# A macaron block of two routed FFN halves around attention: side tasks on even steps, results consumed one step later, head and tail in a new order

## The chip, the cores and the metric

The kernel runs on one core of one Trainium2 chip. Its time is the device time of one execution in microseconds. The core has a matmul engine (TensorE, PE in the profile; its weight loads are PEld), two elementwise engines that read the matmul results from PSUM (VectorE, DVE; ScalarE, ACT), a third elementwise engine (GpSimd, POOL), and a queue (SyncE, SP) that only issues DMAs. Each engine works through its own instruction list in order; semaphores tie the lists together.

## The reference, cut to what matters

```
x = L0_attn_x                                       # (4, 512, 512)
x = x + 0.5 * ffn(layernorm(x))
x = x + attn(layernorm(x))                          # 32 query heads, 8 key/value groups, head size 128
x = x + 0.5 * ffn(layernorm(x))

attn: q, k = rope(x@Wq), rope(x@Wk);  v = x@Wv
      out = softmax(causal(q k^T / sqrt(128))) v;   return out @ Wo + bo
ffn:  query = h@Wq.T;  scores = (query@Wr.T)(aux_keys@Wr.T).T / sqrt(48) + log_rel      # 128 slots
      top 8 of the slots; w = softmax of their (query.key / 8 + log_rel)
      aux = (w @ values) @ Wvd.T @ Wvu.T
      u = log1p(var(h)) / mean(log1p(var(h))) * 0.5 + sigmoid(gelu(h@Wu1.T + bu1)@Wu2.T + bu2) * 2.5
      gate = sigmoid(gate_w1 * clip((clip(u,0,5) - 0.5)/1.5, 0, 1) + gate_bias), 0 where under 0.05
      return h + gate * aux
```

## The kernel before

All of x stays in SBUF as X, 16 tiles of 128 rows by 512 columns, four tiles to a batch. Every product is made of three 16-bit matmuls (a high part and a low part of each operand, `mm3`, the lines L1047, L1048 and L1049), so almost every PSUM result is read twice: ScalarE copies the high part out, VectorE subtracts it to get the low part.

**Steps.** Attention runs as 128 steps s: 4 batches, 8 groups (a unit n is one group of one batch, 32 in all), 4 heads h, so s = 4n + h. In step s TensorE does, in this order: scores(s) (L1202 to L1204, into SC); the query projection of the head two steps on (`queries_of`); attend(s-2) (into PV), which needs the probabilities of two steps ago, turned by DMA; the side tasks of this step (`side`); and the rest (`rest_of`): at h = 1 the next unit's K projection, at h = 3 its V projection, and in every step one of the four row tiles of a unit's output projection O.

**What the other engines do in a step.** VectorE, in order: minima(s) (mask and row minimum, L863), the low parts of the probabilities of step s-1 (`p_lo`, L874, four pieces, with the reciprocal L955 among them), the rope of the query (L834 to L836), `out_lo(s-2)` (L881), then the rest of the same step, thus K's rope, or V's low part (L840), and the add of O into X (`project_add`, L850), and at the end the side tasks. ScalarE: exps(s) (L565), `out_hi(s-2)` (L557), `p_hi(s)` (L574), the high parts of the ropes (L547) and of V (L551), side tasks, and in the first batch the high parts of the weights (L541). GpSimd: the two additions of every rope (L436, L439), side tasks, and in the first batch the low parts of the weights (L429), a second subtraction over 128x512. SP: refills of weights, and for each step four transposing DMAs (`turn`, L374), each when VectorE has written that piece's low part.

**PSUM.** Every projection and every side task writes one of four banks (PJ) in turn: `RING` is the list of all those tasks in TensorE's order, and a task waits (`free`) until the task four places before it has been read (`consumed`).

**Side tasks.** While batch b is in attention, the first FFN half of batch b+1 (tables ending in _A) and the second half of batch b-1 (_B) run in between. The tables are keyed by the step within the batch, u = 0 to 31. LT turns a normalised tile (L1060) and is followed by ScalarE's high part (`hi`) and VectorE's low part (`lo`, L718); SCR, HID, HOUT, ET and AUX are the router scores, the hidden layer, its output, the turned softmax (L1099) and the product with the values. `nrm` (L712) normalises a tile, `aux` (L820) adds the FFN's result to X, `mom` (L678) takes its moments.

**Head and tail.** Before step 0 come the setup products of the FFN's weights, the first half for batch 0 (`HEAD`) and the first four projections (`FIRST`). Behind step 127 come the last output projections (`LAST`) and the second half for batch 3, with all 16 AUX products of that half (`TAIL`). In the head every engine waits for all 14 small loads at once:

```
            pe.wait_ge(ld_f, 16 * NFL)
            mm(PV[0:RDIM, 0:NSLOT], fwrT[:, :], fkeyT[:, :], start=True, stop=True).then_inc(fs_pe, 1)
```

## Time and profile before

| | us |
|---|---|
| median of 3 runs (1540.57 to 1544.21) | 1541.02 |
| the profiled execution | 1551.33 |
| its span, from the first to the last instruction | 1549.5 |
| TensorE busy | 1420.2 |
| VectorE busy | 1222.1 |
| ScalarE busy | 882.3 |
| GpSimd busy | 527.7 |

The profile is of one execution. Busy is the time in which an engine had an instruction under way; the rest is idle, and the profile says which event ended an idle time. The granted clock is TensorE's clock as a share of 2.4 GHz: 0.5 is the level of 1.2 GHz. A row of the timeline merges instructions of one line that follow each other (x4), and gives in brackets the idle time before the first and what ended it.

### The profile page before, as it was taken

Reading aid. Unit: us, or ns where it says so; the run is one execution under the profiler, and the core shown is the slowest. Engines: PE = TensorE matmul, PEld = TensorE weight load, DVE = VectorE, ACT = ScalarE, POOL = GpSimd, SP = SyncE. Lnnn points to the kernel's source line nnn. Section 1 sums busy time; section 2 is a strip of 40 time slices with the busy share of each in tenths; the row PEclk is TensorE's granted clock in tenths of the full one; section 3 lists DMA queues with packets and bytes.
Section 4 is the critical chain, followed back from the end, with each engine's and each line's share of the span. In section 5 each row is a group of like instructions: output and inputs, shape, how many; then the busy total and the mean of one; then the engine's idle time right before and its main releaser. Section 6 shows DMA issues by size and latency. Waiting matters only on the chain.

```text
span 1549.5 us, 26280 instructions
## 1 busy us (share of the span) xinstructions
PE 1420.2 (92%) x8962; PEld 800.1 (52%) x8962; DVE 1222.1 (79%) x3119; ACT 882.3 (57%) x2170; POOL 527.7 (34%) x441
## 2 busy tenths in 40 slices
PE   3487998999999999999899999999899999999966
...
GB/s 220 41 67 183 178 156 166 187 188 163 168 140 144 126 118 99 129 115 112 116 139 129 124 106 112 136 107 110 113 139 134 135 133 134 125 113 120 105 52 109
DMA packets 409539, 201.12 MB, mean 130 GB/s; under 512 B 352160, under 2 KB 353376, under 8 KB 409408
## 3 DMA queue, kind: packets, MB, share of 16 engines
...
## 4 chain that ended last, share of the span: by engine, by line
PE 70%; DVE 13%; ACT 6%; issue 4%; POOL 3%; SPq 2%; DMA 2%; POOLq 0%; ACTq 0%; DVEq 0%
PE PJ L1047 16%; PE PJ L1049 16%; PE PJ L1048 16%; PE PV L1047 4%; PE PV L1049 4%; PE PV L1048 4%; PE SC L1202 3%; PE SC L1203 3%; PE SC L1204 3%; ACT p L565 3%; DVE phl L874 2%; POOL t L436 2%; DVE p L863 2%; DMA pTf<-phl 1%; DVE t L836 1%
## 5 line engine op out<-in xcount | busy, mean ns | idle before, releaser
L436 POOL TENSOR_TENSOR t<-t 128x512 f32<-128x512 f32 x160 | 202.9, 1268 | 744.5 <-DVE t L836 744.3
L565 ACT ACTIVATE p<-p,mn 128x512 f32<-128x512 f32 (+3 forms) x512 | 281.7, 553 | 191.2 <-DVE mn L863 191.0
L874 DVE SCALAR_TENSOR_TENSOR phl<-p,ri,phl 128x512 f16<-128x512 f32 (+3 forms) x512 | 292.7, 595 | 0.0
L574 ACT ACTIVATE phl<-p,ri 128x512 f16<-128x512 f32 (+3 forms) x512 | 245.1, 552 | 14.8 <-DVE ri L959 12.0
L1047 PE MATMUL PJ<-XTh,wsp 128*128 128x512 f16 x640 | 244.3, 382 | 1.4 <-DVE XTl L718 1.4
L1048 PE MATMUL PJ<-XTl,wsp 128*128 128x512 f16 x640 | 244.1, 381 | 0.0
L1049 PE MATMUL PJ<-XTh,wsp 128*128 128x512 f16 x640 | 244.1, 381 | 0.0
L1047 PE MATMUL PJ<-wosp,oTf 128*128 128x512 bf16 x512 | 197.4, 386 | 29.8 <-issue 24.4
L863 DVE CUSTOM_DVE_ANT_0 p<-SC,maskw 128x512 f32<-128x512 f32 (+3 forms) x512 | 220.0, 485 | 4.9 <-PE SC L1204 3.1
L1049 PE MATMUL PJ<-wosp,oTl 128*128 128x512 bf16 x512 | 197.7, 386 | 0.0
L1048 PE MATMUL PJ<-wosp,oTf 128*128 128x512 f16 x512 | 197.3, 385 | 0.0
L1047 PE MATMUL PV<-pTf,vh 128*128 128x512 f16 (+3 forms) x512 | 157.0, 307 | 26.6 <-DMA pTf<-phl 26.6
L439 POOL TENSOR_TENSOR qTl<-t,qTh 128x512 f16<-128x512 f32 x128 | 148.2, 1158 | 94.3 <-ACT qTh L547 94.3
L547 ACT CAST qTh<-t 128x512 bf16<-128x512 f32 x128 | 79.1, 618 | 150.3 <-POOL t L436 150.3
L850 DVE TENSOR_TENSOR X<-PJ,X 128x512 f32<-128x512 f32 x128 | 88.1, 689 | 93.0 <-PE PJ L1049 93.0
L1048 PE MATMUL PV<-pTf,vh 128*128 128x512 f16 (+3 forms) x512 | 157.2, 307 | 0.0
L1203 PE MATMUL SC<-kTl,qTh 128*128 128x512 f16 (+3 forms) x512 | 154.1, 301 | 0.0
L1049 PE MATMUL PV<-pTf,vl 128*128 128x512 f16 (+3 forms) x512 | 150.9, 307 | 0.0
L1202 PE MATMUL SC<-kTh,qTh 128*128 128x512 bf16 (+3 forms) x512 | 147.8, 302 | 2.8 <-POOL qTl L439 2.8
L1204 PE MATMUL SC<-kTh,qTl 128*128 128x512 bf16 (+3 forms) x512 | 147.3, 300 | 0.0
L557 ACT ACTIVATE oTf<-PV 128x512 bf16<-128x512 f32 x128 | 75.6, 591 | 114.1 <-PE PV L1049 114.0
L1049 PEld LDWEIGHTS PJ<-XTh,wsp 128*128 128x128 f16 x640 | 62.9, 98 | 76.6 <-issue 2.1
...
## 6 DMA issues: line engine op xcount, KB each, us to landing
...
pTf<-phl SPq DMA_TRANSPOSE x512, 2.9
...
```

The source lines that it names most:

```text
L436: nc.gpsimd.tensor_tensor(t1[:, j, :], t1[:, j, :], t2[:, j, :], ALU.add).then_inc(rope_sum, 1)
L439: nc.gpsimd.tensor_tensor(lo, t1[:, j, :], hi, ALU.subtract).then_inc(rope_lo, 1)
L565: ins = nc.scalar.activation(pt, pt, ACT.Exp, bias=mn[:, par, i:i + 1], scale=-1.0, accum_out=rs[:, par, i:i + 1])
L574: nc.scalar.activation(phl[:, par, POFF[i]:POFF[i] + w], p[:, par, SOFF[i]:SOFF[i] + w], ACT.Copy, scale=ri[:, par, i:i + 1]).then_inc(a_p ...
L863: ins = nc.vector.tensor_tensor_reduce(out=p[:, par, SOFF[i]:SOFF[i] + w], in0=SCf[:, SOFF[i]:SOFF[i] + w], in1=maskw[:, T - w:T], scale=1 ...
L874: nc.vector.scalar_tensor_tensor(out=phl[:, par, POFF[i] + w:POFF[i] + 2 * w], in0=p[:, par, SOFF[i]:SOFF[i] + w], scalar=ri[:, par, i:i + 1],
L1047: mm(out_, lh, rh, start=start, stop=False)
L1048: mm(out_, lh, rl, start=False, stop=False)
L1049: return mm(out_, ll, rh, start=False, stop=stop)
L1202: mm(o, qh, kh, start=True, stop=False)
L1203: mm(o, qh, kl, start=False, stop=False)
L1204: ins = mm(o, ql, kh, start=False, stop=True)
```

## The change

Five things change together.

- VectorE, ScalarE and GpSimd take what TensorE projected in the rest of step s (K, V, O) in step s+1 (`rest_before`), ahead of the query's rope; TensorE's own order keeps K at h = 1 and V at h = 3, and O comes one step later than before, so the wait for `o_lo` of a unit's last head stands at h = 2.
- TensorE's side tasks stand on even steps alone, mostly two at a time. Tiles go through two buffers per half (`hb` and the unused `asc`).
- The head: the small loads have five semaphores in the order of use and the weights' loads wait for the third quarter of x; the products for the scores come first, those for the values behind the first turned tiles; the moments of tiles 4 to 15 are spread between other work on VectorE; GpSimd's penalty goes before the weights' low parts and its bias adds behind the first ropes; ScalarE spreads the weights' high parts; V's projection goes behind the first query's.
- The end of the loop: the last unit's output projections do three of four heads before the last attend, and the fourth behind it.
- The tail: the hidden layer goes first, the gates of all 16 tiles are made in one pass, VectorE takes tile 15 too, and the last quarter of the output is stored as two halves.

```diff
-PE_A = {2: [("LT", 0, 0)], 3: [("LT", 0, 1)], 4: [("LT", 0, 2)], 6: [("LT", 0, 3)], 7: [("SCR", 0, 0)],
-        8: [("HID", 0, 0)], 10: [("SCR", 0, 1)], 11: [("HOUT", 0, 0)], 14: [("ET", 0, 0)],
-        16: [("AUX", 0, 0)], 18: [("AUX", 0, 1)], 19: [("AUX", 0, 2)], 20: [("AUX", 0, 3)],
-        23: [("LT", 1, 0)], 24: [("LT", 1, 1)], 26: [("LT", 1, 2)], 27: [("LT", 1, 3)]}
-PE_B = {9: [("LT", 2, 0)], 12: [("LT", 2, 1)], 13: [("LT", 2, 2)], 15: [("LT", 2, 3)], 17: [("SCR", 1, 0)],
-        18: [("HID", 1, 0)], 21: [("SCR", 1, 1)], 22: [("HOUT", 1, 0)], 25: [("ET", 1, 0)]}
...
+PE_A = {2: [("LT", 0, 0), ("LT", 0, 1)], 4: [("LT", 0, 2), ("LT", 0, 3)], 6: [("SCR", 0, 0)], 8: [("SCR", 0, 1)],
+        10: [("HID", 0, 0)], 12: [("HOUT", 0, 0), ("ET", 0, 0)], 18: [("AUX", 0, 0), ("AUX", 0, 1)],
+        20: [("AUX", 0, 2), ("AUX", 0, 3)], 24: [("LT", 1, 0), ("LT", 1, 1)], 26: [("LT", 1, 2), ("LT", 1, 3)]}
+PE_B = {12: [("LT", 2, 0), ("LT", 2, 1)], 14: [("LT", 2, 2), ("LT", 2, 3)], 16: [("SCR", 1, 0)], 22: [("SCR", 1, 1)],
+        28: [("HID", 1, 0)], 30: [("ET", 1, 0), ("HOUT", 1, 0)]}
...
+DVE_A = {0: [("nrm", 0, 0), ("nrm", 0, 1)], 2: [("lo", 0, 0), ("lo", 0, 1), ("nrm", 0, 2), ("nrm", 0, 3)],
+         4: [("lo", 0, 2), ("lo", 0, 3)], 6: [("scr", 0, 0)], 7: [("top", 0, 0)], 8: [("scr", 0, 1)],
+         9: [("top", 0, 1)], 10: [("min", 0, 0)], 12: [("hout", 0, 0), ("g1", 0, 0), ("et", 0, 0)],
+         14: [("g2", 0, 0)], 16: [("g3", 0, 0)],
+         18: [("aux", 0, 0), ("mom", 1, 0), ("aux", 0, 1), ("mom", 1, 1)],
+         20: [("aux", 0, 2), ("mom", 1, 2), ("aux", 0, 3), ("mom", 1, 3), ("var", 1, 0)],
+         22: [("std", 1, 0), ("nrm", 1, 0), ("nrm", 1, 1)],
+         24: [("lo", 1, 0), ("lo", 1, 1), ("nrm", 1, 2), ("nrm", 1, 3)], 26: [("lo", 1, 2), ("lo", 1, 3)]}
...
+def rest_before(s):
+    return rest_of(*divmod(s - 1, HG)) if s else []
+
+
 def queries_of(n, h):
     q = (n, h + 2) if h < 2 else (n + 1, h - 2)
     return [("Q",) + q + (0,)] if q[0] < NU else []
 
 
 def rest_of(n, h):
-    r = {0: [("O", n - 2, 3, 0)], 1: [("K", n + 1, 0, 0), ("O", n - 1, 0, 0)], 2: [("O", n - 1, 1, 0)],
-         3: [("V", n + 1, 0, 0), ("O", n - 1, 2, 0)]}[h]
+    r = {0: [("O", n - 2, 2, 0)], 1: [("K", n + 1, 0, 0), ("O", n - 2, 3, 0)], 2: [("O", n - 1, 0, 0)],
+         3: [("V", n + 1, 0, 0), ("O", n - 1, 1, 0)]}[h]
     return [t for t in r if 0 <= t[1] < NU]
...
-FIRST = [("K", 0, 0, 0), ("V", 0, 0, 0), ("Q", 0, 0, 0), ("Q", 0, 1, 0)]
-LAST = [("O", NU - 2, 3, 0)] + [("O", NU - 1, i, 0) for i in range(4)]
...
+FIRST = [("K", 0, 0, 0), ("Q", 0, 0, 0), ("V", 0, 0, 0), ("Q", 0, 1, 0)]
+LAST = [("O", NU - 2, 2, 0), ("O", NU - 2, 3, 0)] + [("O", NU - 1, i, 0) for i in range(4)]
+TAIL = ([("LT", 2, 3, i) for i in range(4)] + [("HID", 1, 3, 0), ("MEAN", 1, 0, 0), ("SCR", 1, 3, 0), ("SCR", 1, 3, 1),
+        ("HOUT", 1, 3, 0)] + [("AUX", 1, 0, i) for i in range(4)] + [("AUX", 1, 1, 0), ("AUX", 1, 1, 1), ("ET", 1, 3, 0),
+        ("AUX", 1, 1, 2), ("AUX", 1, 1, 3)] + [("AUX", 1, b, i) for b in range(2, 4) for i in range(4)])
...
-REFILL = {0: [(1, "Q1"), (1, "V")], 1: [(1, "Q2"), (0, "W0")], 2: [(1, "Q3"), (2, "K"), (0, "W1")],
-          3: [(2, "Q0"), (0, "W2"), (0, "W3")]}
-HEAD_ITEMS = [(0, "K"), (0, "V"), (0, "Q0"), (0, "Q1"), (0, "Q2"), (0, "Q3"), (1, "K")]
+REFILL = {0: [(1, "Q1"), (1, "V"), (-1, "W3")], 1: [(1, "Q2")], 2: [(1, "Q3"), (2, "K"), (0, "W0")],
+          3: [(2, "Q0"), (0, "W1"), (0, "W2")]}
+HEAD_ITEMS = [(0, "K"), (0, "Q0"), (0, "V"), (0, "Q1"), (0, "Q2"), (0, "Q3"), (1, "K")]
...
+            for dst, src in ((fwrT[:, :], f_wrT), (fkeyT[:, :], f_keyT), (fwr[:, :], f_wr)):
+                sp.dma_start(dst, src).then_inc(ld_fr, 16)
+            sp.dma_start(fwq, f_wq).then_inc(ld_fq, 16)
+            sp.dma_start(fwu1T, f_wu1T.rearrange("(c p) n -> p c n", p=P)).then_inc(ld_fu, 16)
+            for dst, src in ((fvalT, f_valT.rearrange("(c p) n -> p c n", p=P)),
+                             (fwvdT[:, :, :], f_wvdT.rearrange("(c p) n -> p c n", p=P)), (fwvuT, f_wvuT)):
+                sp.dma_start(dst, src).then_inc(ld_fv, 16)
...
+            sp.wait_ge(ld_x[2], 16)
+            for r in range(4):
+                raw_load(r)
+            for dst, src in ((ck[:, :], cosk), (sk[:, :], sink), (cq[:, :], cosq), (sq[:, :], sinq),
+                             (bob[:, :], bo.to_broadcast([P, C]))):
                 sp.dma_start(dst, src).then_inc(ld_t, 16)
...
+            for c0, c1 in ((0, 4), (4, 8), (8, 12), (12, 14), (14, 16)):
+                sp.wait_ge(r_xd[1], evens(c1))
+                sp.wait_ge(r_xp[1], c1 - evens(c1))
+                sp.dma_start(out_v[:, c0:c1, :], X[:, c0:c1, :]).then_inc(st_out, 16)
+            sp.wait_ge(st_out, 16 * 5)
...
+            penalty(0, 0)
             for r in range(6):
                 weight_low(r)
-            penalty(0, 0)
-            for i in range(4):
-                add_bias(0, i)
             for kind, n, idx, _ in FIRST:
                 if kind in "QK":
                     rope(kind, n, idx)
             weight_low(6)
+            for i in range(4):
+                add_bias(0, i)
...
-            act.wait_ge(ld_f, 16 * NFL)
+            for c in range(CC):
+                act.wait_ge(fs_pe, 3 + c)
+                nc.scalar.copy(ah[:, c, :], setup_bank(c)).then_inc(fs_hi, 1)
+            root(0, 0, 0, 4)
+            act.wait_ge(ld_fu, 16)
             nc.scalar.copy(uh[:, :, :], fwu1T).then_inc(fs_hi, 1)
-            for c in range(CC):
-                act.wait_ge(fs_pe, 5 + c)
-                nc.scalar.copy(ah[:, c, :], SC[:, c % 2, 0:2 * NSLOT]).then_inc(fs_hi, 1)
...
             for i in range(4):
                 turned_hi(0, 0, i)
+            act.wait_ge(fs_pe, 8)
+            nc.scalar.copy(v2h[:, :], PV[:, :]).then_inc(fs_hi, 1)
+            for i in range(4):
                 base(0, 0, i)
+            act.wait_ge(ld_fs, 96)
+            gelu(0, 0)
+            logs(0)
+            exps_ffn(0, 0)
+            weight_high(0)
+            e_hi(0, 0)
...
             root(0, 1, 4, NT)
-            logs(0)
-            gelu(0, 0)
-            for r in range(6):
-                weight_high(r)
-            exps_ffn(0, 0)
-            gate_exp(0, 0, 4)
-            e_hi(0, 0)
-            gate_exp(1, 0, 4)
+            weight_high(2)
             root(1, 0, 0, 4)
+            weight_high(3)
             for i in range(4):
                 turned_hi(1, 0, i)
+            weight_high(4)
+            weight_high(5)
...
+                for kind, m, _, _ in rest_before(s):
+                    if kind == "V":
+                        value_hi(m)
                 if s >= 2:
                     out_hi(s - 2)
                 p_hi(s)
-                for kind, m, idx, _ in queries_of(n, h) + rest_of(n, h):
-                    if kind in "QK":
-                        rope(kind, m, idx)
-                    if kind == "V":
-                        value_hi(m)
+                for kind, m, _, _ in rest_before(s):
+                    if kind == "K":
+                        rope("K", m, 0)
+                for _, m, idx, _ in queries_of(n, h):
+                    rope("Q", m, idx)
...
+            gelu(1, bb)
             for i in range(4):
                 base(2, bb, i)
-            gelu(1, bb)
+            gate_exp(8, 0, NT)
+            gate_exp(9, 0, NT)
...
+            dve.wait_ge(fs_pe, 2)
+            nc.vector.tensor_copy(rmat[:, :], PJ[0:BOT, 2, 0:NSLOT]).then_inc(fs_ev, 1)
             for n in range(4):
-                moments(0, n)
...
+                setup_lo(c)
             deviation(0, 0, 0, 4)
             for i in range(4):
                 normal(0, 0, i)
...
                 turned_lo(0, 0, i)
...
+            dve.wait_ge(fs_pe, 7)
+            nc.vector.tensor_copy(u1T[:, :], SC[0:VB, 0, 0:NSLOT]).then_inc(fs_ev, 1)
+            dve.wait_ge(ld_fs, 96)
+            for n in range(6, 10):
+                arrived(n)
+            take_scores(0, 0, 0)
+            top(0, 0, 0)
+            arrived(10)
+            take_scores(0, 0, 1)
+            top(0, 0, 1)
+            for n in range(11, NT):
+                arrived(n)
             variance(0, 4, NT)
             dve.wait_ge(ln_v[0], 2)
             variance_logs(0)
...
+            minima_ffn(0, 0)
+            dve.wait_ge(fs_hi, 6)
+            nc.vector.tensor_tensor(v2l[:, :], PV[:, :], v2h[:, :], ALU.subtract).then_inc(fs_lo, 1)
...
+            e_lo(0, 0)
             gate_2(0, 0, 0, 4)
-            e_lo(0, 0)
-            gate_3(0, 1, 0, 4, 1)
+            gate_3(0, 1, 0, 4)
+            scales(0, 0, 4, 1)
...
                 nc.vector.tensor_scalar_mul(ri[:, par, :], ri0[:, :], PSCALE).then_inc(d_norm, 1)
                 if s:
                     p_lo(s - 1, 3)
-                for kind, m, idx, _ in queries_of(n, h):
-                    rope(kind, m, idx)
-                if s >= 2:
-                    out_lo(s - 2)
-                for kind, m, idx, _ in rest_of(n, h):
+                for kind, m, idx, _ in rest_before(s):
                     if kind == "K":
                         rope(kind, m, idx)
                     if kind == "V":
                         value_lo(m)
                     if kind == "O":
                         project_add(m, idx)
+                for kind, m, idx, _ in queries_of(n, h):
+                    rope(kind, m, idx)
+                if s >= 2:
+                    out_lo(s - 2)
...
+            for _, m, idx, _ in rest_before(NS):
+                project_add(m, idx)
             for k in range(TB):
                 p_lo(NS - 1, k)
             out_lo(NS - 2)
+            for _, n, i, _ in LAST[:2]:
+                project_add(n, i)
             out_lo(NS - 1)
-            for _, n, i, _ in LAST:
+            for _, n, i, _ in LAST[2:]:
                 project_add(n, i)
...
+            learned(1, bb)
+            gate_1(1, 0, NT, 4)
             top(1, bb, 0)
+            gate_2(1, 8, 0, NT)
             take_scores(1, bb, 1)
...
+            gate_3(1, 9, 0, NT)
+            scales(1, 0, 12, 3)
...
+            for n in (6, 8, 10, 12, 14, 15):
...
+            pe.wait_ge(ld_fr, 48)
+            mm(PJ[0:RDIM, 3, 0:NSLOT], fwrT[:, :], fkeyT[:, :], start=True, stop=True).then_inc(fs_pe, 1)
             pe.wait_ge(fs_ev, 1)
-            mm(SC[0:BOT, 2, 0:NSLOT], fwr[:, :], rk[:, :], start=True, stop=True).then_inc(fs_pe, 1)
+            mm(PJ[0:BOT, 2, 0:NSLOT], fwr[:, :], rk[:, :], start=True, stop=True).then_inc(fs_pe, 1)
...
+            for c in range(CC):
+                mm(setup_bank(c)[:, 0:NSLOT], fwq[:, c * P:(c + 1) * P], rmat[:, :], start=True, stop=True)
+                mm(setup_bank(c)[:, NSLOT:2 * NSLOT], fwq[:, c * P:(c + 1) * P], fkeyT[:, :],
+                   start=True, stop=True).then_inc(fs_pe, 1)
+            pe.wait_ge(cst, 1)
+            for task in HEAD[:4]:
+                ffn_task(task)
+            pe.wait_ge(fs_lo, 4)
+            pe.wait_ge(ld_fv, 48)
...
+            for task in HEAD[4:6]:
+                ffn_task(task)
             pe.wait_ge(fs_ev, 3)
-            for c in range(CC):
-                if c >= 2:
-                    pe.wait_ge(fs_lo, c)
-                mm(SC[:, c % 2, 0:NSLOT], fwq[:, c * P:(c + 1) * P], rmat[:, :], start=True, stop=True)
...
+            pe.wait_ge(fs_lo, 5)
+            ffn_task(HEAD[6])
+            pe.wait_ge(ld_fs, 96)
...
+            for kind, n, idx, _ in LAST[:2]:
                 project(kind, n, idx)
+            pe.wait_ge(o_lo, NS - 1)
+            for h in range(HG):
+                piece_ready(NU - 1, f"W{h}")
+            for task in LAST[2:]:
+                free(task)
+                project_out(NU - 1, task[2], range(HG - 1))
             attend(NS - 1)
-            for kind, n, idx, _ in LAST[1:]:
-                project(kind, n, idx)
+            pe.wait_ge(o_lo, NS)
+            for task in LAST[2:]:
+                project_out(NU - 1, task[2], range(HG - 1, HG)).then_inc(s_o, 1)
```

## Rows read from the trace of the kernel before

**Rows 1.** Stretches: length, busy of PE, PEld, DVE, ACT, POOL; clock, DMA share, GB/s.
```profile
0.00:99.17 99.17, 47.50 (x233) 29.89 (x233) 51.38 (x142) 26.50 (x49) 20.13 (x25) 0.83 0.30 102
99.17:164.38 65.21, 52.23 (x288) 28.52 (x289) 51.70 (x116) 44.38 (x106) 37.04 (x31) 0.87 0.69 174
164.38:455.09 290.71, 275.32 (x1761) 152.98 (x1760) 248.97 (x581) 187.68 (x461) 157.71 (x130) 0.98 0.68 169
455.09:807.39 352.30, 341.40 (x2221) 193.72 (x2220) 289.55 (x753) 206.54 (x516) 106.12 (x88) 1.00 0.52 123
807.39:1161.59 354.20, 344.09 (x2221) 194.50 (x2220) 289.23 (x753) 206.53 (x516) 104.26 (x86) 0.99 0.53 119
1161.59:1470.31 308.72, 307.00 (x1985) 172.47 (x1984) 251.55 (x658) 183.06 (x469) 91.07 (x75) 1.00 0.55 125
1470.31:1508.18 37.87, 25.95 (x122) 12.05 (x120) 17.81 (x48) 9.51 (x21) 0.00 (x0) 0.91 0.28 59
1508.18:1549.50 41.32, 26.75 (x138) 15.92 (x138) 21.91 (x69) 18.07 (x33) 11.40 (x9) 0.79 0.28 102
```

**Rows 2.** TensorE's waits, whole span: line, released by: us in total, times, longest.
```profile
PE PV L1047 <- DMA pTf<-phl: 26.6, 13, 4.5
PE PJ L1047 <- issue: 24.4, 13, 3.9
PE PV L1209 <- DMA lrb<-in_f_lr: 21.3, 1, 21.3
```

**Rows 3.** VectorE's waits, whole span.
```profile
DVE X L850 <- PE PJ L1049: 93.0, 84, 3.7
DVE vl L840 <- ACT vh L551: 58.7, 32, 2.5
```

**Rows 4.** Stretch of one unit without side tasks (steps 96 to 99).
```profile
1161.59:1200.62 39.03, 39.03 (x253) 21.62 (x252) 32.62 (x82) 22.14 (x58) 12.15 (x10) 1.00 0.56 135
```

**Rows 5.** The page: turning DMAs, count, us from issue to landing.
```profile
pTf<-phl SPq DMA_TRANSPOSE x512, 2.9
```

**Rows 6.** Timeline from step 104's to step 105's minima: start, us, engine, line, operation.
```profile
1242.74 0.69 DVE L863 CUSTOM_DVE_ANT_0 p<-SC,maskw 128x512 f32<-128x512 f32 x1
...
1244.38 1.28 DVE L874 SCALAR_TENSOR_TENSOR phl<-p,ri,phl 128x512 f16<-128x512 f32 x2
...
1249.92 0.68 DVE L863 CUSTOM_DVE_ANT_0 p<-SC,maskw 128x512 f32<-128x512 f32 x1
...
1245.16 5.40 SPq L374 DMA_TRANSPOSE pTf<-phl  x4
```

**Rows 7.** DMA issues of the head: count, KB each, median us to landing.
```profile
fkeyT<-in_f_keyT SPq DMA_DIRECT2D x1, 32.0 KB, 7.4
```

**Rows 8.** Timeline of the head, all engines; in brackets the idle time before.
```profile
35.44 3.65 PE L1060 MATMUL PJ<-ident,pTf 128*128 128x128 f32 x16 [4.02 <-DVE pTf L712]
...
41.35 7.21 DVE L678 BATCH_NORM_STATS2 st<-X 128x6 f32<-128x512 f32 x12
...
51.49 1.28 ACT L510 ACT_TABLE_LOAD   x1
...
52.79 0.69 ACT L510 ACTIVATE gT<-PJ,bu 128x512 f32<-128x512 f32 x1
...
54.07 6.96 POOL L429 TENSOR_TENSOR wsp<-raw,wsp 128x512 f16<-128x512 f32 x6 [51.74 <-ACT wsp L541]
...
82.88 0.58 PE L1047 MATMUL PJ<-XTh,wsp 128*128 128x512 f16 x1 [1.45 <-DVE XTl L718]
...
99.17 0.61 PE L1202 MATMUL SC<-kTh,qTh 128*128 128x512 bf16 x1 [2.82 <-POOL qTl L439]
```

**Rows 9.** VectorE's low parts in batch 0, GpSimd busy with weights.
```profile
246.65 2.87 DVE L874 SCALAR_TENSOR_TENSOR phl<-p,ri,phl 128x512 f16<-128x512 f32 x2
```

**Rows 10.** Timeline of the tail: GpSimd's last adds into X.
```profile
1540.36 3.85 POOL L467 TENSOR_TENSOR X<-X,t 128x512 f32<-128x512 f32 x3 [1.25 <-ACT t L657]
```

More of the change, by code:

```diff
@@ new lines @@
+DVE_B = {6: [("var", 2, 0)], 8: [("std", 2, 0), ("nrm", 2, 0), ("nrm", 2, 1)],
+         12: [("lo", 2, 0), ("lo", 2, 1), ("nrm", 2, 2), ("nrm", 2, 3)], 14: [("lo", 2, 2), ("lo", 2, 3)],
+         16: [("scr", 1, 0)], 17: [("top", 1, 0)], 22: [("scr", 1, 1)], 23: [("top", 1, 1)], 24: [("min", 1, 0)],
+         30: [("et", 1, 0), ("hout", 1, 0)]}
+ACT_A = {2: [("hi", 0, 0), ("hi", 0, 1)], 3: [("xup", 0, 0), ("xup", 0, 1)], 4: [("hi", 0, 2), ("hi", 0, 3)],
+         5: [("xup", 0, 2), ("xup", 0, 3)], 10: [("gelu", 0, 0)], 11: [("exp", 0, 0)], 12: [("et", 0, 0)],
+         13: [("gexp", 0, 0)], 15: [("gexp", 0, 1)], 21: [("root", 1, 0)], 24: [("hi", 1, 0), ("hi", 1, 1)],
+         26: [("hi", 1, 2), ("hi", 1, 3)]}
@@ L124, in refills @@
     out = [(1, "Q0")] if s == 0 else []
-    return out + [(n + d, kind) for d, kind in REFILL[h] if n + d < NU]
+    if s == NS - 1:
+        out = [(NU - 1, "W3")]
+    return out + [(n + d, kind) for d, kind in REFILL[h] if 0 <= n + d < NU]
 ITEMS = list(HEAD_ITEMS)
@@ L260, in rope_index, with evens @@
             return 5 * n if kind == "K" else 5 * n + idx + 1
+        odd = [1, 3, 5, 7, 9, 11, 13]
         def odd_tile(f, n):
-            return f == 1 and n % 2 == 1
+            return f == 1 and n in odd
+        def evens(n):
+            return n - len([m for m in odd if m < n])
         def consumed(task):
@@ L469, in _ @@
             penalty(1, B - 1)
-            for n in range(1, NT, 2):
+            for n in odd:
                 aux_add(n)
@@ L613, in _ @@
                 p_hi(s)
-                for kind, m, idx, _ in queries_of(n, h) + rest_of(n, h):
-                    if kind in "QK":
-                        rope(kind, m, idx)
-                    if kind == "V":
-                        value_hi(m)
+                for kind, m, _, _ in rest_before(s):
+                    if kind == "K":
+                        rope("K", m, 0)
+                for _, m, idx, _ in queries_of(n, h):
+                    rope("Q", m, idx)
                 for stage, k, bb, i in side(ACT_A, ACT_B, s):
@@ L658, in aux_odd @@
                                      scale=gs[:, 1, n:n + 1]).then_inc(r_xa[1], 1)
-            for n in range(1, 8, 2):
+            for n in odd[:3]:
                 aux_odd(n)
             exps_ffn(1, bb)
-            gate_exp(10, 12, NT)
             e_hi(1, bb)
-            gate_exp(11, 12, NT)
-            for n in range(9, NT, 2):
+            for n in odd[3:]:
                 aux_odd(n)
@@ L906, in _ @@
                 normal(0, 0, i)
+            dve.wait_ge(fs_hi, 5)
+            nc.vector.tensor_tensor(ul[:, :, :], fwu1T, uh[:, :, :], ALU.subtract).then_inc(fs_lo, 1)
+            arrived(4)
+            arrived(5)
             for i in range(4):
                 turned_lo(0, 0, i)
-            for n in range(4, NT):
-                if n % 4 == 0:
-                    dve.wait_ge(ld_x[n // 4], 16)
-                moments(0, n)
+            dve.wait_ge(fs_pe, 7)
[9 more added lines that the diff above has]
+            for n in range(11, NT):
+                arrived(n)
             variance(0, 4, NT)
@@ L1134, in halves, with project_out @@
                 return w[:, 0, :].bitcast(BF16), w[:, 1, :]
+            def project_out(n, idx, heads):
+                ts = lo_slice(idx)
+                for h in heads:
+                    wh, wl = halves(f"W{h}", n)
+                    ins = mm3(bank(("O", n, idx, 0)), oTh[:, n % 2, h, ts], oTl[:, n % 2, h, ts], wh, wl,
+                              h == 0, h == HG - 1)
+                return ins
             def project(kind, n, idx):
```

171 lines of the change are left out of this document (64 added, 107 removed).

## The prediction, made before the changed kernel was run

> **What bounds the kernel now.** I read the busy time by stretch first, then who waited for whom, then the timeline of the worst places. TensorE is busy 1420 of 1549.5 us (the PE column of [rows 1] added up), 92%, so only the rest of the span and the time at the slow clock can be won. I cut the span at the first scores of steps 0, 6, 32, 64, 96 and 127 and at the tail's first turned tile. The loss of a stretch is its idle time plus its length times (1 - granted clock), since at 1.2 GHz work takes twice as long. By [rows 1] that is, for steps 0 to 5, 13.0 + 8.5 = 21.5 us; steps 6 to 31, 15.4 + 5.8 = 21.2; batch 1, 10.9 (its clock is 1.00 as rounded); batch 2, 10.1 + 3.5 = 13.6; batch 3, 1.7; from step 127 to the tail 11.9 + 3.4 = 15.3; together 84. The head before step 0 is 99.2 us with TensorE busy for 47.5, and the tail 41.3. Thus some 225 us lie outside TensorE's bound; the middle is at it: a unit without side tasks takes 39.03 us with TensorE busy for 39.03 [rows 4].
>
> The waits say why the loop loses. TensorE waits 26.6 us for turned probabilities, and 24.4 us under "issue" at first matmuls of output projections, the longest 3.9 us [rows 2]. VectorE waits 93.0 us for the O it has to add, in 84 places, and 58.7 us at V's low part for ScalarE's high part [rows 3]. TensorE makes both at the end of a step, so an in-order engine stands still behind them, with side tasks and the next minima queued. VectorE is busy 32.6 of the 39.0 us of a clean unit [rows 4] and 290 of 352 in batch 1 [rows 1]: once it has stood still it is late, `out_lo` too, and two steps on the probabilities are late.
>
> **Units of time.** A clean unit is 180 matmuls of 512 columns or their equal (4 scores and 4 attends of 7.5 each, 10 projections of 12), so one is 39.03 / 180 = 0.217 us [rows 4], a projection 2.6, scores or an attend 1.6. Even steps are 8.4, odd ones, with K or V, 11.1. VectorE's step is 1249.92 - 1242.74 = 7.2 us if nothing waits [rows 6]: rope 2.1 (three of 0.7), `out_lo` 0.6, an add 0.6, and 3.9 for minima and low parts.
>
> **Part A, the head up to step 0.** The first product needs fkeyT, fwrT and fwr. These are now the first three issues; fkeyT takes 7.4 us from issue to landing [rows 7], so about 8.7 us in place of 21.3 [rows 2]. From there to the first turned tile it is 35.4 - 21.3 = 14.1 us now [rows 8]. The value products leave this path, four moments join it, as no waiting hides them any more (7.21 / 12 = 0.6 each, 2.4 in all [rows 8]); I count 9.3, so the tile comes at 18.0 and 17.4 is gained. From the tile to K's first matmul it is 82.9 - 35.4 = 47.4 us now. Twelve moments leave the path (7.2) and six weight subtractions ahead of the penalty (7.0) [rows 8]. Back come five moments and their sums (3.9, I take all of it), the router scores at the slow clock (3.9 of the up to 5.2 that 48 matmuls of 256 columns can lose), and 3.0 for the order gelu, logs, exps and the gates one behind the other: net 3.4. Query before V takes one projection, 2.6, off the way to the first scores. Sum 23.4; I take 22, range 12 to 27: a load that lands late would cut it.
>
> The switch of a function table on ScalarE shows as 1.28 us and the gelu follows at once: 51.49 + 1.28 = 52.77, and it starts at 52.79 [rows 8]. The Trainium skill ("ScalarE: Activation LUTs", What ACT_TABLE_LOAD costs) says that a switch costs about 2.66 us, as a drain follows the load. That rule speaks against the new order, which puts three switches between the hidden layer and the softmax: by it part A would gain 4 us less and the kernel come out at 1483. The trace shows no such drain, so the sum does not hold it.
>
> **Part B, steps 0 to 5.** VectorE is busy 51.7 of 65.2 us [rows 1] while the pipeline fills. In the change its waits for V's high part, up to 2.5 us each [rows 3], and for O go, and one O moves to the end. Of the 21.5 lost I leave 14.5, a gain of 7. Bounds: 0 if the chain of scores, exps, low parts and DMA is all there is, 14 if only the slow clock's part stays.
>
> **Part C, steps 6 to 31.** The same, with weights prepared beside it. Two low parts take 2.87 us while GpSimd subtracts, against 1.28 [rows 6, 9]. Every subtraction stays (6.96 / 6 = 1.16 each [rows 8]), and at h = 2 GpSimd now holds two ropes and three weights, about 2 x 2.4 + 3 x 1.16 = 8.3 us, which reaches into the next step's low parts. So VectorE stays near the bound: of 21.2 I leave 9, a gain of 12, range 5 to 18.
>
> Two low parts beside GpSimd's subtraction are the slower by 1.6 us [rows 6, 9]. The Trainium skill ("GPSIMD Engine Reference", 8. Key points) says GpSimd shares its SBUF interfaces with VectorE and contends with instructions of two SBUF inputs, which the low parts are. The trace agrees; if that contention alone made C's loss, all of it would stay and the kernel would come out at 1491.
>
> **Part D, batches 1 to 3.** K's rope adds 2.1 to VectorE's step and V's low part 0.6; a pair of tiles adds 1.2 for `lo`, 0.9 for `nrm`, and some 2.3 of waiting for ScalarE. At h = 2 with two tiles VectorE needs 7.2 + 2.1 + 2.1 + 2.3 = 13.7 against TensorE's 9.3, and is 4.4 late; the odd step gives back 11.1 - 7.2 = 3.9. The turning DMAs begin 2.4 us behind the minima, take 5.4 to issue and 2.9 from the last one's issue to landing: 2.4 + 5.4 - 1.35 + 2.9 = 9.4 [rows 5, 6]. TensorE wants them 4.2 into the next step, so it notices a lateness of over 12.6 - 9.4 = 3.2 us in an even step and 5.9 in an odd one. So the old waits go. New are waits in the ring of four banks, as a bank is freed a step later. At h = 2 the second tile needs K's bank, read 0.9 + 3.9 + 2.1 = 6.9 us into the step, when TensorE wants it at 1.6 + 2.6 + 1.6 + 0.5 = 6.3; with O behind it this costs 0.8, four or five times a batch. At u = 12 the ring is Q, LT, LT, HOUT, ET, O: O needs the first tile's low part, which follows the query's rope on VectorE (8.1), GpSimd (1.3) and ScalarE (2 x 0.6), at 10.6, where TensorE wants it at 8.0: with ET's wait 3 us. That makes 6 to 7 a batch, against 10.9 and 13.6 now and up to 2 of clock that the rounding hides. Gain 7 in each less 2 for batch 3, which has next to nothing to give: 12 in all, range 0 to 24.
>
> **Part E, step 127 to the tail, 37.9 us.** 15.3 of it is lost [rows 1]. Ahead of attend(127) TensorE now has three heads of the last four O, 4 x 9 x 0.217 = 7.8 us, which covers a wait for probabilities (at most 4.5 [rows 2]); behind it VectorE is the limit with four adds and four moments, 4 x 1.3. One O of 2.6 more is done here. I take 5, range 1 to 9.
>
> **Part F, the tail, 41.3 us.** GpSimd's last add ends at 1540.36 + 3.85 = 1544.2 [rows 10] and the last store takes the 5.3 us to the end. Half its size saves about 1.3; one add fewer on GpSimd (3.85 / 3 = 1.3) and one gate pass fewer (1.5) help; but the gates now wait for the hidden layer. I take 4, range -2 to 8.
>
> **Sum.** 22 + 7 + 12 + 12 + 5 + 4 = 62. Against its own execution: 1551.3 - 62 = 1489.3, with a span of 1487.5. The median of the runs is 10.3 under the profiled execution, so 1541 - 62 = 1479.
>
> **The rivals.**
> The loop gives nothing: each wait removed comes back as a bank's, or VectorE catches up and waits for O as before, which is also the case in which the change does not do what it says. For it: u = 12 and the contention of batch 0. Against: 151 us of VectorE's waits are for results that will be a step old. Left are A + E + F = 31: 1510.
>
> The loop gives nearly all: VectorE's 6.4 us of slack a unit take up the side work. B 12, C 19, D 22, with A 22 and 14 for E and F: 89, thus 1452.
>
> The head gives half: a load or ScalarE's order eats it, A 10: 1491.
>
> Slower: K's rope (2.1) and an add (0.6) now stand in an even step ahead of the query's rope; if VectorE enters even steps over 3.2 us late, each unit pays these 2.7 us on TensorE's path: 31 x 2.7 = 84 less the 62, thus 1563. For it: 4.4 late and 3.9 back do not quite cancel. Against: units with two pairs of tiles are few, and a clean one gives back more.
>
> **How the numbers follow.** Forecast 58%, loop nothing 12%, loop all 17%, head half 10%, slower 3%. The likeliest is 1479. The range of 1450 to 1512 holds all but the slower case and the outer parts of the others, some 15%. Measurement tells 0.3%, 4.6 us, from no change: faster 0.965, same 0.01, slower 0.025.
>
> **What would show it.** The first product at about 9 us and the first scores at 75 to 80 (A). VectorE's waits at the add of O and at V's low part nearly gone, and no long "issue" at O (B to D); batches 1 and 2 at 343 to 347 us each, with a wait at u = 12 that VectorE's `lo` ends (D); no wait at attend(127) (E). It is wrong if the first scores come after 87 us, or if batches 1 and 2 stay over 350 or come out at 339, where only their work is left.

## The result

The changed kernel takes 1529.25 us (median of 4 runs, 1528.1 to 1531.99) against 1541.65 for the kernel before: ratio 0.992, 95% interval 0.9901 to 0.9939, clear of the noise though under 1%. It is 12 us faster where 62 were forecast, and outside the range of 1450 to 1512. The profiled execution took 1528.1 us with a span of 1525.9.

I cut the changed kernel's span at the same places as [rows 1]: first scores of steps 0, 6, 32, 64, 96 and 127, and the tail's first turned tile.

Stretches of the changed kernel: length, busy of PE, PEld, DVE, ACT, POOL; clock, DMA share, GB/s.
```profile
0.00:72.48 72.48, 40.12 (x232) 27.79 (x235) 50.19 (x140) 26.58 (x49) 14.52 (x20) 0.86 0.42 140
72.48:136.42 63.94, 48.68 (x277) 27.64 (x280) 50.63 (x115) 42.53 (x103) 39.97 (x32) 0.89 0.65 161
136.42:431.32 294.90, 272.07 (x1729) 151.58 (x1755) 262.96 (x584) 185.94 (x460) 161.03 (x129) 0.98 0.71 169
431.32:783.78 352.46, 340.84 (x2190) 193.88 (x2221) 293.89 (x754) 206.92 (x520) 110.01 (x90) 0.99 0.54 123
783.78:1136.22 352.44, 340.54 (x2189) 193.68 (x2220) 290.96 (x753) 205.10 (x517) 104.65 (x86) 0.99 0.55 120
1136.22:1444.59 308.37, 305.47 (x1954) 172.28 (x1984) 255.59 (x658) 183.59 (x472) 93.51 (x76) 1.00 0.57 126
1444.59:1483.22 38.63, 26.71 (x131) 12.80 (x132) 18.76 (x51) 8.87 (x19) 0.00 (x0) 0.91 0.26 60
1483.22:1525.90 42.68, 25.43 (x136) 15.57 (x138) 20.31 (x57) 15.64 (x29) 10.10 (x8) 0.86 0.27 99
```
Against [rows 1] the head gave 26.7 us and steps 0 to 5 gave 1.3. Steps 6 to 31 took back 4.2. Batch 1 stands still, batch 2 gave 1.8, batch 3 0.3, and the last two stretches took back 2.1. The sum is 23.6, the whole difference of the two spans; the medians differ by 12, as the profiled execution of before was a long one. A second one of the same kernel had a head of 95.2, 289.0 us for steps 6 to 31 and a span of 1543.7, so read single stretches to 2 us, and the head to 4.

In the loop the waits of [rows 2] and [rows 3] are nearly gone, as forecast, and others stand in their place.

Waits of the changed kernel, whole span: us in total, times, longest. TensorE first (left out: 19.1 us, in the head and tail, for VectorE to normalise tiles), then VectorE, and last VectorE's wait for the scores in the kernel before.
```profile
PE PV L1102 <- DMA pTf<-phl: 18.2, 11, 3.2
PE PJ L1268 <- DMA fwr<-in_f_wr: 9.3, 1, 9.3
PE PJ L1115 <- DVE t L877: 7.9, 8, 1.7
PE PJ L1102 <- DVE t L877: 6.5, 4, 3.8
PE PJ L1115 <- DVE vl L881: 6.0, 3, 3.4
PE PJ L1103 <- DVE raw L756: 5.9, 2, 2.9
PE PJ L1154 <- DVE vl L881: 4.0, 1, 4.0
...
DVE p L904 <- PE SC L1263: 97.6, 57, 3.8
DVE ri L1007 <- ACT p L588: 57.5, 38, 4.9
DVE X L891 <- PE PJ L1104: 6.2, 4, 2.1
```
```profile
DVE p L863 <- PE SC L1204: 3.1, 3, 2.2
```
L1115 turns a tile, L1154 turns the scores, L1102 begins a projection and L1103 is another of its three matmuls. The last five of TensorE's lines are waits for a bank of PJ that VectorE has not finished reading: after K's rope (t, L877), V's low part (vl, L881), a tile's low part (raw, L756). VectorE's waiting did not vanish either. It moved from O (93.0 us, now 6.2) and V's high part (58.7, now 3.1) to the scores (3.1, now 97.6) and ScalarE's exps (19.8, now 57.5).

The costliest kind of step is that with h = 2 and two tiles. Step 58 (u = 26 of batch 1) starts at 717.51. Timeline of TensorE, then VectorE: start, us, engine, line, operation; in brackets the idle time before and its releaser.
```profile
723.37 0.61 PE L1115 MATMUL PJ<-ident,hb 128*128 128x128 f32 x4
725.70 0.65 PE L1115 MATMUL PJ<-ident,asc 128*128 128x128 f32 x4 [1.73 <-DVE t L877]
726.65 0.38 PE L1103 MATMUL PJ<-wosp,oTf 128*128 128x512 f16 x1 [0.30 <-DVE X L891]
```
```profile
718.47 0.69 DVE L904 CUSTOM_DVE_ANT_0 p<-SC,maskw 128x512 f32<-128x512 f32 x1 [0.75 <-PE SC L1263]
...
722.76 0.18 DVE L1007 RECIPROCAL ri<-rs 128x4 f32<-128x4 f32 x1 [1.36 <-ACT p L588]
...
724.96 0.68 DVE L877 TENSOR_TENSOR t<-PJ,sk 64x512 f32<-64x512 f32 x1
725.67 0.69 DVE L891 TENSOR_TENSOR X<-PJ,X 128x512 f32<-128x512 f32 x1
```
K was ready before the step began. Its bank is read to the end at 725.64, 8.1 us into the step; VectorE stood idle for 0.75 us before the minima and for 1.36 before the reciprocal, with K's rope queued behind both.

### The profile page after: what moved, and what is told of

Its sections match the earlier page's. It is cut to its first block, busy times and chain, and to the rows that moved or that the text cites. A ratio compares the mean times of both kernels' runs of the same rounds, so it can differ in the third digit from the quotient of the medians.

```text
span 1525.9 us, 26148 instructions
## 1 busy us (share of the span) xinstructions
PE 1399.9 (92%) x8832; PEld 795.2 (52%) x8962; DVE 1243.3 (81%) x3107; ACT 875.2 (57%) x2166; POOL 533.8 (35%) x440
## 4 chain that ended last, share of the span: by engine, by line
PE 61%; DVE 19%; ACT 11%; issue 4%; POOL 4%; DMA 1%; SPq 0%; DVEq 0%; ACTq 0%
PE PJ L1103 15%; PE PJ L1104 14%; PE PJ L1102 13%; ACT p L588 5%; DVE phl L915 3%; POOL t L457 3%; PE SC L1263 3%; PE SC L1261 3%; PE SC L1262 3%; PE PV L1102 3%; PE PV L1104 3%; PE PV L1103 3%; DVE p L904 2%; DVE t L877 2%; DVE t L876 2%
## 5 line engine op out<-in xcount | busy, mean ns | idle before, releaser
L915 DVE SCALAR_TENSOR_TENSOR phl<-p,ri,phl 128x512 f16<-128x512 f32 (+3 forms) x512 | 315.9, 640 | 0.0
L904 DVE CUSTOM_DVE_ANT_0 p<-SC,maskw 128x512 f32<-128x512 f32 (+3 forms) x512 | 220.1, 486 | 98.0 <-PE SC L1263 97.6
L1102 PE MATMUL PJ<-XTh,wsp 128*128 128x512 f16 x640 | 243.1, 380 | 3.4 <-DVE t L877 1.6
L1103 PE MATMUL PJ<-XTl,wsp 128*128 128x512 f16 x640 | 242.8, 379 | 0.0
L1103 PE MATMUL PJ<-wosp,oTf 128*128 128x512 f16 x512 | 197.9, 387 | 16.5 <-DVE raw L756 5.9
L1104 PE MATMUL PJ<-wosp,oTl 128*128 128x512 bf16 x492 | 190.0, 386 | 0.0
L1102 PE MATMUL PV<-pTf,vh 128*128 128x512 f16 (+3 forms) x512 | 154.1, 301 | 19.5 <-DMA pTf<-phl 18.2
L1102 PE MATMUL PJ<-wosp,oTf 128*128 128x512 bf16 x415 | 160.4, 387 | 2.5 <-DVE oTl L922 1.4
L1103 PE MATMUL PV<-pTf,vh 128*128 128x512 f16 (+3 forms) x512 | 154.5, 302 | 0.0
L922 DVE SCALAR_TENSOR_TENSOR oTl<-PV,oTf 128x512 f16<-128x512 f32 x128 | 88.6, 692 | 16.7 <-ACT oTf L580 12.8
```

The source lines that it names most:

```text
L904: ins = nc.vector.tensor_tensor_reduce(out=p[:, par, SOFF[i]:SOFF[i] + w], in0=SCf[:, SOFF[i]:SOFF[i] + w], in1=maskw[:, T - w:T], scale=1 ...
L915: nc.vector.scalar_tensor_tensor(out=phl[:, par, POFF[i] + w:POFF[i] + 2 * w], in0=p[:, par, SOFF[i]:SOFF[i] + w], scalar=ri[:, par, i:i + 1],
L1102: mm(out_, lh, rh, start=start, stop=False)
L1103: mm(out_, lh, rl, start=False, stop=False)
L1104: return mm(out_, ll, rh, start=False, stop=stop)
```

## The experiments

My theory after the result: the loop gains nothing because results are consumed behind the minima and low parts of the next step, so that banks come free late. Rival: VectorE, or its contention with GpSimd, has no room for even steps with two tiles. Each ratio is to the kernel before, timed beside the run.

**The kernel before again.** Nothing edited.

> The kernel before, unchanged, for a second profile and to see how far a profiled execution may lie from the median. If the first profile of it (1551.3 us) was an outlier of some 10 us, this one should show about 1541 with the difference in batch 0, where the traffic is heaviest; if profiling itself costs 10 us, it shows 1551 again.

Measured: 1543.94 us, ratio 1.0012 (0.9992 to 1.0032). Batches 1 and 2 take 352.9 and 353.8 us.

**The old loop.** Tables, `rest_of`, REFILL and the reading of K, V and O of the kernel before; head and tail new:
```
-for kind, m, idx, _ in rest_before(s): ...   # ahead of the query's rope
 for kind, m, idx, _ in queries_of(n, h): rope(kind, m, idx)
 if s >= 2: out_lo(s - 2)
+for kind, m, idx, _ in rest_of(n, h): ...    # behind out_lo, in the same step
```
The even-step tables and the late reading are taken back together here; no run takes back the tables alone.

> The changed kernel with the loop of before (its tables, its one-step-earlier O, its refills, K, V and O read in the step that makes them), but with the new head, the new end and the new tail. Theory 1 (the head carries the whole gain and the new loop loses in batch 0 what it wins nowhere): 1541 - 27 + 1 = 1515, first scores at about 73 us, batches 1 and 2 at 352 each as before, steps 6 to 31 at 291. Theory 2 (the new loop is worth the 12 us and the head's gain is lost elsewhere): 1530 or more.

Measured: 1524.79 us, ratio 0.9881 (0.9852 to 0.991). The kernel without the new loop is no slower than the changed one: the loop's part is worth 0, or less. The stretches agree: 67.8, 287.0, 354.2 and 352.2 us for steps 0 to 5, steps 6 to 31 and batches 1 and 2. So with the head and tail alike, the new loop gives 3.8 us in steps 0 to 5 and 1.7 in batch 1, and loses 7.9 in steps 6 to 31.

**Table A's tasks first** (the two appends in `side` change places, so that at u = 12 HOUT and ET come ahead of the two tiles).

> The changed kernel with the order of the side tasks within a step turned: those of the first half (HOUT, ET) before those of the second (LT, LT), on all engines. It matters at u = 12 alone, where the output projection takes the bank of the first LT and waits for its low part, 2.95 us and then the slow clock. Bank theory: step 12 of batches 1 and 2 falls from 17 to about 11.5 us, so 10 to 11 us in all: 1518. Rival (VectorE is late there anyway and the wait moves to the next step): less than 3 us, 1527 or more.

Measured: 1524.43 us, ratio 0.9874 (0.9845 to 0.9903). Step 12 of batch 1 falls from 17.24 to 12.38 us, that of batch 2 from 16.92 to 13.80. The mechanism at u = 12 is right, but at u = 24 and 26 the steps grow by 0.6 to 2.0 us each, so that of 8.0 us the two batches keep 4.6. The whole gives 5 us: neither the 11 of the theory nor the under 3 of its rival.

**The old tail** (four stores, eight odd tiles on GpSimd, gates in two passes).

> The changed kernel with the tail of before (order of the tasks, two gate passes, eight adds on GpSimd, four stores). By the two profiles the tail is 41.3 us before and 42.7 after, so 1.4 us faster than the changed kernel: 1528. By my prediction the new tail saves 4: 1533.

Measured: 1527.52 us, ratio 0.9896 (0.9868 to 0.9924), and 80.5 us from step 127 to the end against 81.3. The new tail gives nothing.

**No weight subtractions**, in the changed kernel and in the one before:
```
-nc.gpsimd.tensor_tensor(w[:, 1, :], raw[:, r % NRAW, :], w[:, 0, :].bitcast(BF16), ALU.subtract)...
+nc.gpsimd.memset(w[:, 1, :], 0.0)...
```

> The changed kernel with GpSimd's subtraction for the low parts of the weights (1.16 us each, batch 0 and the head) replaced by a fill with zeros, so the low halves of all weights are left out; nothing else moves. Theory: steps 6 to 31 grew to 294.9 us because the side work now stands in even steps, where these subtractions slow VectorE's low parts. Then steps 6 to 31 fall by 8 to 12 us, to 283 to 287, batches 1 to 3 stay within 1 us, and the kernel comes to 1513 to 1520. Rival, VectorE has too much to do in the even steps of its own: steps 6 to 31 stay at 292 to 295 and the kernel at 1526 to 1529.

> The kernel before with the same subtractions replaced by zeros (the low halves of the weights are left out). Theory that contention hurts the new loop more than the old: steps 6 to 31 of before fall less, from 289 or 290.7 to about 284 to 286, and both kernels meet there. Rival, the contention is the same in both: both fall by the same amount and the 5 us between them stay.

Measured: 1513.35 us, ratio 0.9807 (0.9785 to 0.9828), and 1534.02, ratio 0.9934 (0.9911 to 0.9957). Steps 6 to 31 are 284.1 us long in both. The time of VectorE's low parts in these steps shows a part of the reason. The same view for the four kernels, in the order changed, changed without subtractions, before, before without them: length, VectorE's and ScalarE's busy time on phl (count), clock, DMA share, GB/s.
```profile
136.42:431.32 294.90, 83.50 (x104) 50.66 (x107) 0.98 0.71 169
```
```profile
131.69:415.81 284.12, 61.82 (x105) 51.59 (x108) 0.99 0.75 176
```
```profile
164.38:455.09 290.71, 74.45 (x104) 49.83 (x104) 0.98 0.68 169
```
```profile
157.65:441.77 284.12, 54.45 (x104) 49.71 (x104) 0.99 0.69 173
```
The subtractions lengthen the low parts by 21.7 us in the changed kernel and by 20.0 in the one before, so about equally. But they cost 10.8 us of time in the one and 6.6 (4.9 by its second profile) in the other: in the changed kernel the reads that free K's and V's banks stand behind the lengthened low parts. TensorE's waits for VectorE to free a bank bear this out: in these steps they come to 15.1 us, and to 8.7 without the subtractions.

What is not separated: a fill takes 0.52 us where the subtraction took 1.16, so these runs also shorten GpSimd's own queue. No wait of TensorE or VectorE in these steps is ended by GpSimd, but ScalarE waits 64.6 us there for its additions to the query's rope (56.8 without the subtractions), so a share of the 10.8 may come that way. A second rise of the low parts, of 7.4 us, is left between the two kernels without subtractions, though both take 284.1 us. I put it down to GpSimd's part of the ropes, now with K's beside the low parts; no run takes those away.

**O read first**, then **K and O first**, then **K, V and O first.** On VectorE:
```
+for kind, m, idx, _ in rest_before(s):       # K and O (the first of these kernels: O alone)
+    if kind == "K": rope(kind, m, idx)
+    if kind == "O": project_add(m, idx)
 minima(s)
+for kind, m, idx, _ in rest_before(s):       # third kernel only; on ScalarE value_hi goes ahead of exps(s)
+    if kind == "V": value_lo(m)
 if s:
     p_lo(s - 1, 0)
...
```
Their old places, behind the low parts, are gone.

> The changed kernel, but VectorE adds the O made one step ago before it takes the minima of its own step, where it stands idle for the scores (97.6 us in all), and not behind the four low parts. Theory that banks read late took the place of the old waits: TensorE's waits for an O's read go, about 3 us a batch, and the kernel comes to 1518 to 1523. Rival, VectorE is full: the minima are later by 0.6, the probabilities too, and the time stays at 1528 to 1532.

> The changed kernel with O's add and K's rope ahead of the minima on VectorE, V left where it was. Adding O alone gave 11 us, O, K and V together 30. If K's bank (read 6.9 us into the steps with h = 2, wanted at 6.3) carries the other 19, the kernel comes to 1500 to 1506; if V's bank carries it, read behind the low parts in the steps with h = 0, it comes to 1512 to 1517.

> The changed kernel, but K's rope and O's add stand ahead of the minima on VectorE, V's high part ahead of the exps on ScalarE, V's low part between the minima and the low parts: every bank of the step before is free 2 to 4 us earlier. Theory of the late banks: batches 1 and 2 fall from 352.5 to 343 to 346 each, the kernel to 1505 to 1515. Rival, late probabilities: K's rope (2.1 us) delays the turning, TensorE waits for turned tiles instead, and the kernel stays at 1525 or becomes slower.

Measured, with steps 6 to 31, batch 1 and batch 2 behind the ratio:

| read first | us | ratio | steps 6 to 31 | batch 1 | batch 2 |
|---|---|---|---|---|---|
| nothing (the change) | 1529.25 | 0.992 (0.9901 to 0.9939) | 294.9 | 352.5 | 352.4 |
| O | 1518.13 | 0.9837 (0.9815 to 0.9859) | 288.7 | 349.0 | 350.5 |
| K, O | 1506.08 | 0.9762 (0.9734 to 0.9791) | 286.0 | 346.0 | 346.2 |
| K, V, O | 1498.90 | 0.9715 (0.9693 to 0.9737) | 286.6 | 346.2 | 345.4 |

The same work in another order gives 23 us with VectorE's order alone, and 30 with V too, for which ScalarE's order changes as well. The last is more than the 1505 to 1515 expected. O and K carry the loop's share. That it is the order and not the length of the low parts shows in steps 6 to 31: with K and O first these are still 80.9 us long (83.5 in the change), and the stretch is 8.9 us shorter.

V's step gives 7 us in the medians but nothing in these stretches, and the 3.3 us by which its profile is shorter lie in the head (1.5) and behind step 127 (1.7). In steps 6 to 31 it trades one wait for another: K and O first leaves 7.4 us of waits for V's bank (L881), and with V first they are gone, but the waits for turned probabilities grow. With K and O first, then with V too:
```profile
PE PV L1103 <- DMA pTf<-phl: 4.9, 5, 2.0
```
```profile
PE PV L1103 <- DMA pTf<-phl: 12.6, 9, 4.9
```
So the lateness that the rival feared does come in batch 0, and cancels V's gain there; in batches 1 and 2 it is 4.0 us together.

Step 58 in the third kernel begins at 704.68. Its VectorE:
```profile
704.82 0.68 DVE L877 TENSOR_TENSOR t<-PJ,sk 64x512 f32<-64x512 f32 x1
...
706.14 0.68 DVE L904 CUSTOM_DVE_ANT_0 p<-SC,maskw 128x512 f32<-128x512 f32 x1
...
709.18 0.18 DVE L1015 RECIPROCAL ri<-rs 128x4 f32<-128x4 f32 x1
```
K's bank is free 0.8 us into the step instead of 8.1, the minima begin 1.46 in instead of 0.96, and the wait before the reciprocal is gone, because ScalarE's exps lie under it. The step takes 9.32 us in place of 11.51. And VectorE waits for O again (its waits over the whole span):
```profile
DVE X L891 <- PE PJ L1105: 64.4, 48, 3.5
```
so 64.4 us of it belong to a kernel that is 30 us faster than the one with 6.2.

**Both together**, and the same with the old tail.

> K, V and O read first (as before, 1499) and within a step the first table's side tasks ahead of the second's, so that at u = 12 the two turned tiles come behind HOUT and ET. TensorE's wait of 2.95 us at u = 12 for the first tile's low part goes in batches 1 and 2. If that holds beside the early reads, the kernel comes to 1493 to 1497 (2 batches by 3 to 4 us less the clock); rival, the tiles' low parts then delay the probabilities: 1498 to 1501.

> The kernel of the run before this with the tail of the kernel before (four stores, eight odd tiles on GpSimd, gates in two passes). The new tail measured 81.2 us from step 127 to the end against 80.5 with the old: if the tail's change is worth nothing, this one stands within 3 us of it; if my term of 4 us was hidden by something in the loop, it comes out 3 to 6 us slower.

Measured: 1490.58 us, ratio 0.9655 (0.9632 to 0.9678), and 1487.53, ratio 0.9639 (0.9613 to 0.9664). These beat both kernels, and the first comes in under the 1493 to 1497 expected. The old tail is again no slower, here by 3 us. Batches 1 and 2 of the first take 340.2 and 340.3 us with TensorE busy for 338.7 and 338.9. Step 12 of batch 1, changed kernel first (start of the step 560.69, next 577.93), then this one (546.51, next 557.57):
```profile
569.63 0.66 PE L1154 MATMUL PJ<-ident,asc 128*128 128x128 f32 x4 [0.95 <-DVE t L877]
573.24 0.63 PE L1103 MATMUL PJ<-wosp,oTf 128*128 128x512 f16 x1 [2.95 <-DVE raw L756]
```
```profile
552.36 1.00 PE L1143 MATMUL PJ<-wu2T,gT 128*128 128x1 f32 x8
...
554.97 0.39 PE L1103 MATMUL PJ<-wosp,oTf 128*128 128x512 bf16 x1 [0.20 <-DVE gl L797]
```
Behind the 2.95 us of idleness each matmul is longer (0.63 us against 0.39). The granted clock in three stretches of the changed kernel's step (the column after POOL's): while the tiles are turned, the waits, and the rest:
```profile
566.00:570.00 4.00, 3.05 (x27) 2.58 (x25) 3.94 (x7) 2.40 (x5) 0.34 (x1) 1.00 0.72 128
570.00:573.20 3.20, 0.29 (x3) 0.18 (x3) 1.41 (x3) 2.08 (x4) 2.08 (x2) 0.71 0.29 85
573.20:577.90 4.70, 4.66 (x11) 1.67 (x11) 1.98 (x6) 0.00 (x0) 0.00 (x0) 0.50 0.00 0
```

## Why the prediction was wrong, by its steps

**Part A was right.** First product at 9.3 us (8.7 forecast), first turned tile at 19.0 (18.0), first scores at 72.5, ahead of the 75 to 80. It gave 26.7 us by the first profile of before and 22.7 by the second, where I had 22. By legs: 16.4 and 15.5 us up to the tile (17.4 forecast), 5.6 and 5.4 up to K's first matmul (3.4), 4.7 and 1.9 from there to the scores (2.6). The size is not settled closer than that: by the medians the whole change gave 12 us, and both profiled executions of the kernel before were longer than its median.

The tile, and ScalarE in the changed head, in the order that I had priced at 3.0 us of chain:
```profile
19.00 3.31 PE L1115 MATMUL PJ<-ident,pTf 128*128 128x128 f32 x16 [3.80 <-DVE pTf L750]
33.27 1.28 ACT L533 ACT_TABLE_LOAD   x1
...
35.27 1.28 ACT L538 ACT_TABLE_LOAD   x1
...
36.79 1.28 ACT L544 ACT_TABLE_LOAD   x1
38.09 0.40 ACT L544 ACTIVATE asc<-asc,mnr 128x128 f32<-128x128 f32 x1
```
Three table loads, one for each of three operations that follow one another, take 1.28 us each, and the operation behind a load starts at once (38.09 = 36.79 + 1.28 + 0.02). The rule of the Trainium skill that a switch costs about 2.66 us ("ScalarE: Activation LUTs", What ACT_TABLE_LOAD costs) does not hold here.

**Part B** gave 1.3 of 7, inside its bounds. Against the old loop behind the same head it gave 3.8 (67.8 to 63.9 us): the new head alone makes these steps 2.6 us longer, which my sum did not hold. Without GpSimd's subtractions they fall to 59.3 us (61.3 in the kernel before): so 4.6 us (3.9 before) of what I left as the pipeline's own filling go with the subtractions.

**Part C failed: 12 forecast, 4 to 6 lost, 7.9 against the old loop behind the new head.** The step reads "VectorE stays near the bound: of 21.2 I leave 9". It counted the waits that go and only noted that GpSimd's work "reaches into the next step's low parts". The runs show the price of that: 10.8 us for the weights' subtractions, more than in the kernel before, as bank reads now queue behind the slowed low parts. That is the loss and not the whole miss: without the subtractions both kernels take 284.1 us, so the 12 us of gain are missing there too, and the reason is Part D's. The rival by which contention keeps all of C's loss was closer than my step; even that was too mild. The Trainium skill ("GPSIMD Engine Reference", 8. Key points) names contention with VectorE instructions of two SBUF inputs, and the trace agrees: the low parts take 83.5 us with the subtractions and 61.8 without.

**Part D failed, and it is the central miss.** "That makes 6 to 7 a batch" was 13.8 in batch 1 (352.5 against the 338.7 of TensorE's work); 12.2 of them go when the banks come free early and u = 12 is reordered. By step of batch 1, against the kernel with both together: u = 12 costs 6.2 where I had 3 (waits of 0.95 and 2.95, the rest slow clock, which I had left out); u = 26 2.2 where I had 0.8; u = 2 and 14 1.0 each, near the 0.8; u = 18 and 30 0.6 and 0.8. What my sum lacked for K's bank, "0.9 + 3.9 + 2.1 = 6.9", is VectorE's wait for ScalarE's exps, 1.36 us, ahead of the reciprocal: measured 8.1. The place of each wait was right but for V's bank at u = 4 (1.2 in batch 2), and the size was half of what came. By the same measure the old loop lost 13.6 and 15.5 us in batches 1 and 2 (352.3 and 354.2 less 338.7), so the new 13.8 and 13.7 all but cancel the gain.

Behind it is a mistake of reading. I took the 151.7 us of [rows 3] as evidence for the gain, though VectorE had the slack. Taking them out only moved them to the scores (97.6) and the exps (57.5), while the delay of one step was paid where TensorE needs it: a ring of four banks, each held longer.

**Part E** lost 0.8 where 5 were forecast. TensorE's waits in the two kernels' last stretch, before and after:
```profile
1474.53 0.59 PE L1047 MATMUL PV<-pTf,vh 128*128 128x512 f16 x1 [2.42 <-DMA pTf<-phl]
1481.08 0.38 PE L1047 MATMUL PV<-pTf,vh 128*128 128x512 f16 x1 [0.51 <-DMA pTf<-phl]
1488.66 0.58 PE L1047 MATMUL PV<-pTf,vh 128*128 128x512 f16 x1 [3.20 <-DMA pTf<-phl]
```
```profile
1447.60 0.38 PE L1102 MATMUL PV<-pTf,vh 128*128 128x512 f16 x1 [1.22 <-DMA pTf<-phl]
1454.66 0.38 PE L1102 MATMUL PV<-pTf,vh 128*128 128x512 f16 x1 [2.67 <-DMA pTf<-phl]
...
1483.22 3.35 PE L1115 MATMUL PJ<-ident,pTf 128*128 128x128 f32 x16 [6.34 <-DVE pTf L750]
```
attend(127) waits for nothing any more (3.20 before), as forecast, but attend(126), earlier in the chain, waits 2.2 us more (attend(125), the first line of each, 1.2 less), and the tile waits 6.34 us for VectorE's adds, moments and first normal tile, where it waited 4.32: the limit behind attend(127) that I had named, without a wait of its own in the sum. With the old loop, which does one O fewer here, the same stretch is 34.9 us long: the new order gives 2.9 there, and with one O more (2.6 of work) it is 3.7 longer. That run's tail is 44.4 us long, though, at a clock of 0.77, so from step 127 to the end it takes 79.3, as the kernel before does (79.2).

**Part F** lost 1.4 (4 forecast, lower bound -2). The last adds end 36.4 us behind the tile, where they ended 36.0 behind it before: the gates in one pass and the add fewer on GpSimd bought nothing that shows at the end. On the way TensorE now waits 1.5, 2.8, 3.1 and 2.4 us (for a tile's low part, the scores' and the first add's banks, and ScalarE's softmax), where it waited 0.9 and 6.3. VectorE and GpSimd end together:
```profile
1514.40 5.15 POOL L490 TENSOR_TENSOR X<-X,t 128x512 f32<-128x512 f32 x4 [4.76 <-ACT t L689]
1518.17 1.41 DVE L861 SCALAR_TENSOR_TENSOR X<-PJ,gs,X 128x512 f32<-128x512 f32 x2 [0.55 <-PE PJ L1104]
```
From there to the end it is 1525.9 - 1519.6 = 6.3 us, against 5.3 before. The term "Half its size saves about 1.3" was wrong in its sign. The last store, issue (start, us) and size with us to landing, before and after:
```profile
1544.29 0.37 SPq L400 DMA_DIRECT2D out<-X  x1
out<-X SPq DMA_DIRECT2D x1, 1024.0 KB, 4.5
```
```profile
1520.09 1.26 SPq L421 DMA_DIRECT2D out<-X  x1
out<-X SPq DMA_DIRECT2D x1, 512.0 KB, 5.4
```
The other half (512 KB, issued at 1519.63) lands in 4.5 us, as the whole did. So here half the size saved nothing, and the issue right behind another took 1.26 us instead of 0.37.

The rival "the loop gives nothing" (1510, 12%) was the one that came true, by its first way and for both reasons given for it: waits came back as banks', at u = 12 above all, and C turned negative. Its other way, VectorE waiting for O as before, did not come (6.2 us). Its 1510 was too low because it took the loop for 0 and E and F for 9; measured were -1 for B to D (1.3 - 4.2 + 1.9; -2.1 against the old loop's run) and -2.1 for E and F.

One reading of the opening does not hold either: the "some 225 us" outside TensorE's bound count the head and the tail whole, with 74 us of TensorE's own work in them. No term of the sum uses it.
